# Where the layer norm, turn and router logits of three batches are placed between attention A and the first expert stage

## What is computed

```
x = x + attention_a(layernorm(x))      # linear attention with rotary positions, elu + 1 features
x = x + experts(layernorm(x))          # shared expert + top 2 of 8 routed experts
x = x + attention_b(layernorm(x))      # causal attention with logarithms and softplus
x = x + experts(layernorm(x))          # the same weights again

def experts(xt):                       # xt: 4096 tokens x 128
    shared = (silu(xt @ sg_w.T) * (xt @ su_w.T)) @ sd_w.T
    probs = sigmoid(xt @ router_w.T + routing_bias)
    topk_p, topk_idx = top_k(probs, 2)
    topk_p = topk_p / sum(topk_p)
    # the two chosen experts, each silu(g) * u @ wd, weighted by topk_p
    return shared + routed
```

## Time and profile before

| | |
|---|---|
| median of 3 runs | 1026.67 us (1026.3 to 1032.23) |
| profiled execution | 1028.98 us, its span 1027.1 us |
| mean granted TensorE clock | 0.908 |
| busy: TensorE / its weight load | 80% / 53% |
| busy: VectorE, ScalarE, GpSimd | 72%, 55%, 57% |
| attention A and the shared phase | 0 to about 200 us |
| pairs of the first expert stage | about 200 to 320 us |

### The profile page before, as it was taken

The page is one execution under the profiler, slowest core; times in us unless marked ns, Lnnn a source line. Parts: engine busy times, 40 slices in busy tenths (PEclk is TensorE's granted clock), DMA queues, the critical chain, the costliest instruction groups (busy, mean ns, idle before and its releaser), DMA issues. The chain is left out here.

```text
span 1027.1 us, 19542 instructions
## 1 busy us (share of the span) xinstructions
PE 819.4 (80%) x6459; PEld 545.3 (53%) x6459; DVE 735.8 (72%) x1506; ACT 568.5 (55%) x805; POOL 586.9 (57%) x815
## 2 busy tenths in 40 slices
PE   3887577899986787888888888979796588899890
PEld 2666566799984333333333333333342256799890
DVE  3888745455563658899999998989789646555574
ACT  1454152133334667989898989998763242233230
POOL 2343486881383666666644444455326877788884
PEclk9999588999997878999999999999877688999996
DMA  9990012123338477584737474732210021132444
GB/s 273 300 131 1 16 39 70 54 81 114 101 84 242 124 197 220 150 227 118 234 108 215 116 208 121 224 106 55 70 42 24 32 75 39 40 102 84 132 135 122
DMA packets 114401, 124.00 MB, mean 121 GB/s; under 512 B 13328, under 2 KB 76560, under 8 KB 114176
## 3 DMA queue, kind: packets, MB, share of 16 engines
q1 hardware_dynamic: 96512, 100.80, 36.2%
q0 software_dynamic: 8416, 17.29, 5.4%
q10 hardware_dynamic: 9376, 4.65, 1.6%
HBM read 59.97 MB, written 62.72 MB: 119 GB/s over the span
## 5 line engine op out<-in xcount | busy, mean ns | idle before, releaser
L2070 DVE TENSOR_SCALAR ring_b<-psum 128x1024 int32<-128x1024 int32 x160 | 194.2, 1216 | 24.0 <-PE psum L1765 20.8
L1930 ACT ACTIVATE ring_a<-psum 128x1024 f32<-128x1024 f32 x160 | 162.4, 1021 | 51.0 <-PE psum L1765 45.7
L1936 ACT ACTIVATE ring_b<-ring_b 128x1024 f32<-128x1024 f32 x160 | 168.7, 1055 | 36.5 <-DVE ring_b L2070 36.1
L2198 POOL TENSOR_SCALAR_AFFINE_SELECT ring_b<-ring_b 128x512 f32<-128x512 f32 (+1 forms) x112 | 80.1, 728 | 171.6 <-ACT ring_b L1936 170.9
L1765 PE MATMUL psum<-stacks 32*128 32x128 f32 (+3 forms) x1024 | 98.9, 385 | 66.2 <-DVE ring_b L2070 36.8
L1765 PEld LDWEIGHTS psum<-stacks 32*128 32x128 f32 x1024 | 56.9, 193 | 173.5 <-ACT ring_a L1930 76.6
L2062 DVE TENSOR_SCALAR ring_a<-ring_a 128x1024 f32<-128x1024 f32 x160 | 119.4, 751 | 16.8 <-ACT ring_a L1930 15.0
L949 ACT ACTIVATE ring_b<-psum 128x512 f32<-128x512 f32 x72 | 42.6, 591 | 114.0 <-PE psum L834 88.0
L1818 PE MATMUL psum<-ring_b,values 128*32 128x256 f32 (+3 forms) x1024 | 94.2, 478 | 8.6 <-POOL ring_b L2198 8.6
L1797 PE MATMUL psum<-ring_a,ones_s 128*32 128x256 f32 (+3 forms) x1024 | 92.3, 469 | 9.8 <-POOL ring_a L2198 9.8
L1092 POOL DMA_INDIRECT r_rows<-y_sorted,rows_of x64 | 67.1, 1048 | 51.3 <-DMA y_sorted<-y_out 39.2
(11 more groups left out here) (220 smaller groups left out, 1484.1 us busy)
## 6 DMA issues: line engine op xcount, KB each, us to landing
stack_q<-parts SPq DMA_DIRECT2D x32, 256.0 KB
stack_ky<-parts SPq DMA_DIRECT2D x32, 256.0 KB
stacks<-stack_q SPq DMA_DIRECT2D x64, 128.0 KB
stacks<-stack_ky SPq DMA_DIRECT2D x64, 128.0 KB
stack_k<-parts SPq DMA_DIRECT2D x32, 256.0 KB
stacks<-stack_k SPq DMA_DIRECT2D x64, 128.0 KB
stack_qr<-parts SPq DMA_DIRECT2D x32, 256.0 KB
stacks<-stack_qr SPq DMA_DIRECT2D x64, 128.0 KB
```

Source lines behind the costliest of these rows:

```text
L1930: nc.scalar.activation(exps[:, n % RING, 2 * u:2 * u + 2, :], psum[:, first:first + 2, :], ACT.Exp, scale=SCALE).then_inc(self.exp, 1)
L1936: nc.scalar.activation(part, part, ACT.Ln, bias=1.0).then_inc(self.ln, 1)
L2070: nc.vector.tensor_scalar(ring[:, m % RING, HEADS_B[u][0]:HEADS_B[u][1] + 1, :].bitcast(I32), psum[:, first:first + 2, :].bitcast(I32), 0x ...
L2198: ins = nc.gpsimd.affine_select(out=part, in_=part, pattern=[[0, part.ap[1][1]], [1, 128]], compare_op=ALU.is_ge, fill=0.0, base=0, channe ...
```

## The change

Batches 5, 6 and 7 are handled like batches 1 to 4, in steps 6 to 9 of attention A; only batch 8 stays in the shared phase. `early` becomes 7 for `ffn_1` and with it `first_late` 8 and `scored` 3, so the choice of chunk 1 moves to item 3, ranks, gates, pages and rows to item 4, its page table to item 5. The logits of batch 7 are taken in the shared phase (TensorE at item 1, VectorE at item 2, before `add_shared`). In steps 8 and 9 turn, parts and low part stand behind the attention output. The page table of chunk 0 moves from step 8 to the end of step 9. The powers of batches 5 and 6 are in GpSimd's steps; that of batch 7 comes after 2 sends, that of batch 8 after 12. Batch 8 is normalised on ScalarE behind silu 0, once its bias is there and the logits of batch 7 are taken (the two share a room); its bias is on VectorE behind hidden 0. New waits of TensorE: the turn of batch 6 for the reading of chunk 0's ranks (bank 4), the first down for the logits sum of batch 7, ranks 0 for the logits sum of batch 5. The second expert stage (`led=True`) is unchanged.

```diff
@@ -291,7 +291,7 @@
                 a_project_tokens(pe, 3, w["w_a"][:, 4 * D:5 * D]).then_inc(a_kv, 1)
-            if 1 <= b - AHEAD - 1 <= ffn_1.early:
+            if b <= B and 1 <= b - AHEAD - 1:
                 ffn_1.tensor_logits(pe, b - AHEAD - 1)
@@ -301,14 +301,18 @@
                 a_numerators(pe, b)
-            if b == 8:
+            if b == B:
                 ffn_1.tensor_ranks(pe, 0)
+            if b == B + 1:
+                ffn_1.tensor_logits(pe, b - AHEAD - 1)
             if b < B:
                 a_project_q(pe, b + 1)
-            if 1 <= b - AHEAD <= ffn_1.early:
-                ffn_1.turn(pe, b - AHEAD)
+                if 1 <= b - AHEAD:
+                    ffn_1.turn(pe, b - AHEAD)
             if b > 1:
                 a_output(pe, b)
+            if b >= B:
+                ffn_1.turn(pe, b - AHEAD)
 
@@ -366,7 +370,7 @@
         def a_vector_step(v, b):
-            if 1 <= b - AHEAD <= ffn_1.early:
+            if 1 <= b - AHEAD and b <= B:
                 ffn_1.vector_bias(v, b - AHEAD)
@@ -375,15 +379,17 @@
                 a_rotate(v, b, 1, k_prod, 2, rope_k)
-            if 1 <= b - AHEAD - 1 <= ffn_1.early:
-                ffn_1.vector_logits_of(v, b - AHEAD - 1)
+                if 1 <= b - AHEAD - 1:
+                    ffn_1.vector_logits_of(v, b - AHEAD - 1)
+            else:
+                ffn_1.vector_bias(v, b - AHEAD)
             if b > 1:
...
                 ffn_1.vector_first(v, 0)
-            if b == 8:
+            if b == B:
                 ffn_1.vector_gates(v, 0)
@@ -391,21 +397,22 @@
                 a_feature(v, b, 1, k_prod, k_exp, k_feat)
-            if 1 <= b - AHEAD <= ffn_1.early:
-                ffn_1.vector_low(v, b - AHEAD)
             if b < B:
+                if 1 <= b - AHEAD:
+                    ffn_1.vector_low(v, b - AHEAD)
                 a_rotate_q(v, b + 1)
-            if b == B + 1:
-                ffn_1.vector_bias(v, ffn_1.first_late)
-                ffn_1.vector_stats(v, ffn_1.first_late + 1)
+            else:
+                if b > B:
+                    ffn_1.vector_logits_of(v, b - AHEAD - 1)
             if b > 1:
                 a_add(v, b)
-            if 1 <= b - AHEAD + 1 <= ffn_1.early:
+            if 1 <= b - AHEAD + 1:
                 ffn_1.vector_stats(v, b - AHEAD + 1)
+            if b >= B:
+                ffn_1.vector_low(v, b - AHEAD)
             if b == 7:
                 ffn_1.vector_second(v, 0)
-            if b == 8:
-                ffn_1.vector_stats(v, ffn_1.first_late)
+            if b == B + 1:
                 ffn_1.vector_experts(v, 0)
@@ -442,10 +449,12 @@
                 ffn_1.scalar_exp(a, 0)
-            if 1 <= b - AHEAD <= ffn_1.early:
+            if b < B and 1 <= b - AHEAD:
                 ffn_1.scalar_parts(a, b - AHEAD)
...
                 a_copy_output(a, b)
+            if b >= B:
+                ffn_1.scalar_parts(a, b - AHEAD)
             if b < B:
@@ -467,7 +476,7 @@
                     a_add_turned(p, b + 1, 0)
-                if 1 <= b - AHEAD + 1 <= ffn_1.early:
+                if 1 <= b - AHEAD + 1 and b < B:
                     ffn_1.pool_rstd(p, b - AHEAD + 1)
@@ -478,11 +487,11 @@
                     nc.gpsimd.tensor_tensor(low, whole, high.bitcast(F32), ALU.subtract).then_inc(split_low, 1)
-            sends = (0, 4, 8, 12, 14, 2 * ffn_1.tiles(0))
-            for k in range(len(sends) - 1):
-                ffn_1.send(p, 0, sends[k], sends[k + 1])
-                if ffn_1.first_late + k <= B:
-                    ffn_1.pool_rstd(p, ffn_1.first_late + k)
+            ffn_1.send(p, 0, 0, 2)
+            ffn_1.pool_rstd(p, B - 1)
+            ffn_1.send(p, 0, 2, 12)
+            ffn_1.pool_rstd(p, B)
+            ffn_1.send(p, 0, 12)
 
@@ -579,8 +588,9 @@
                 self.all_pairs, self.all_quads = (PAGES + 1) // 2, (PAGES + 3) // 4
-                self.early = B - chunks[-1]
+                self.early = B - chunks[-1] if led else B - 1
                 self.first_late = self.early + 1
+                self.first_scored = self.first_late if led else self.early
                 self.quads_soon = (2 * chunks[0] * TT - ROUTED + 1) // 4
@@ -711,6 +721,7 @@
                     pe.wait_ge(self.x_low, self.early)
+                    pe.wait_ge(self.logit_ready, self.early)
                     pe.wait_ge(self.chain, self.chain_at(c, RANKS_READ[self.kind(c)]))
@@ -738,6 +749,8 @@
                         pe.wait_ge(self.logit_ready, b - 1)
+                        if not self.led and b == B - AHEAD:
+                            pe.wait_ge(self.chain, self.chain_at(0, RANKS_READ["first"]))
                     elif self.led:
@@ -763,8 +776,8 @@
                 pe.wait_ge(self.chain, self.chain_at(c, CHOSEN))
-                if self.led and c < len(self.chunks) - 1:
-                    pe.wait_ge(self.logit_ready, self.early)
+                if c < len(self.chunks) - 1:
+                    pe.wait_ge(self.logit_ready, self.early if self.led else B - AHEAD - 1)
                 pe.wait_ge(split_low, 1)
@@ -869,7 +882,7 @@
 
-                if self.first_late <= n + self.first_late - 2 <= B:
+                if self.first_scored <= n + self.first_late - 2 <= B:
                     self.tensor_logits(pe, n + self.first_late - 2)
@@ -914,6 +927,8 @@
                 a.wait_ge(self.bias_ready, b)
+                if not self.led and not self.is_early(b):
+                    a.wait_ge(self.logits, self.early)
                 for t in range(TT):
@@ -989,15 +1004,13 @@
                     self.scalar_exp(a, len(self.chunks) - 1)
-                if self.led and self.first_late + n <= B:
+                if self.first_late + n <= B:
                     self.scalar_hat(a, self.first_late + n)
...
                 for n in range(self.offset):
-                    if not self.led and self.first_late + n <= B:
-                        self.scalar_hat(a, self.first_late + n)
                     self.shared_silu(a, self.shared_first[n // IC], n % IC)
@@ -1541,15 +1554,13 @@
                 b = n + self.first_late - 3
-                if self.first_late <= b <= B:
+                if self.first_scored <= b <= B:
                     self.vector_logits_of(v, b)
...
                 last = len(self.chunks) - 1
-                ahead = self.first_late + n + (1 if self.led else 2)
-                if not self.led and ahead - 1 <= B:
-                    self.vector_bias(v, ahead - 1)
+                ahead = self.first_late + n + 1
                 if ahead <= B:
@@ -1571,11 +1582,16 @@
                     self.shared_hidden(v, b, c)
+                    if not self.led and late + n <= B:
+                        self.vector_bias(v, late + n)
                     if self.led and n == 0:
                         self.previous.finish_vector(v)
+                    if not self.led:
+                        self.late_logits(v, n)
                     if n > 0 and c == 0:
                         self.add_shared(v, b - 1)
-                    self.late_logits(v, n)
+                    if self.led:
+                        self.late_logits(v, n)
                     self.late_vector(v, n)
```

## The result

The changed kernel takes 1034.73 us (median of 20 runs, 1030.56 to 1041.31), the kernel before 1028.99 us (20 runs beside it, 1026.11 to 1038.52). The medians differ by 5.7 us; the estimated ratio is 1.0043, 95% interval 1.0022 to 1.0064, that is 4.4 us slower (2.3 to 6.6). The changed kernel is slower, and clear of the scatter, but by less than the 1% that the prediction took as the bound. The profiled execution took 1040.34 us, its span 1038.5 us, one of the slowest of the 20; so its stages are read one by one and not its length.

The account below looks back on a forecast made before the run. VectorE bounds attention, then TensorE's waits and lower clock set when pairs begin; 8 us gained at the choice is given back, +1.5 us on 1026.67 us gives 1028 us, range 1017.5 to 1035.5 us.

Parts of the forecast that it names:

- Steps 6 to 8: Attention, VectorE: step 6 +1.4 us, step 7 +2.4 us, −4.7 us page table and +0.9 us before ninth head mask.
- First gate-up: Start of the shared phase on TensorE, after logits 6 and batch 7's turn: 131.6 against 130.45 us, so +1.2 us.
- GpSimd: Batch 8's power after twelve sends done at 140.9 us; second half's sends resume at 174.5 us, 3.9 us sooner than before.
- New wait at the turn of batch 8: Shared phase, TensorE: waits 7 us, until 142.9 us, for batch 8's normalisation, held by its bias behind GpSimd's power.
- Ranks: Choice of experts ends and ranks are released at 161.6 us, 8 us sooner than before.
- Row numbers behind down 2: Item 4, VectorE: row numbers late by down 2 (3.5 us) and its sum, done at 174.3 us.
- down 3 to 176.9 us: Shared phase, TensorE: down 3, after item 5's hidden product at 174.9 us, ends at 176.9 us.
- Gate-ups 0 and 1: TensorE has done them and logits 7 by 135.9 us; twelve gate-up matmuls take 3.51 us at the full clock.
- A: Clock stays up in steps 8 and 9 as idle pieces shrink: some 6 us less, 1022 us; chance 0.20.
- B: Clock stays down in the shared phase between its waits until 180 us: 8.9 us more, 1037 us; chance 0.11.
- C: Shared-phase chain is shorter than reckoned, batch 8's power or row numbers sooner: gain some 10 us, 1017 us; chance 0.12.
- Behind it: After the first quad: GpSimd's 3.9 us hidden by pairs' slack of some 3.7 us; clearing of value room taken as nothing.

Follow-up runs that it names:

- all four edits: Changed kernel with batch 8's power after 8 sends, page table in item 2, rows before batch 2's sum, batch 7's logit sum in item 1: ratio 0.9949.
- two other kernels: Changed kernel with power after 8 sends, page table in item 2, rows before batch 2's sum, without and with logit sum in item 1: ratios 0.9945, 0.9949.

## Why the prediction was right, and where not

*Overall.* The prediction was 1028 us, +1.5 us over the kernel before; measured were 1034.73 us and +4.4 us by the ratio, in the range and within 1%. Of the 6.7 us between 1028 and 1034.73, 2.3 us are the base (1026.67 us, the median of three runs, where twenty gave 1028.99). The reason was right: what the chain gains, it gives back at the wait for batch 8 and at the row numbers. At the first quad, where the sum ends, the two pairs of profiles show +4.3 and +0.1 us, 2.2 on the mean, against +1.5. The rest of the slowdown lies where the prediction had nothing, or in the scatter; its cause is open.

*Steps 6 to 8.* Right. Step 6 +1.4 us: 12.79 against 11.39 where the clock was up in both profiles. Step 7 +2.4: measured 1.8. Step 8 −3.8: measured −3.77 in the first pair of profiles, −2.7 in the second (13.92 against 16.61 us), where the clock stayed up longer in the kernel before. Head mask of step 8 at 109.2 (108.0), of step 9 at 123.8 (122.6). VectorE sets these steps, and its instructions could be summed.

*First gate-up* +1.2 us: it came at 132.61 and 131.96 against 130.45 and 132.22 us, less than the scatter.

*GpSimd.* Power of batch 8 done at 142.03 us (140.9), the first hidden product just ahead of it at 140.04. Right, and shown by moving it. The second half's sends start at 176.41 us, 1.9 us sooner than before and not 3.9, behind 2.91 us of idle time where almost none was expected: 1.4 us is the late row numbers, and the sum left 0.2 us between row numbers and the first send where both kernels have 0.76.

*New wait at the turn of batch 8.* 6.14 us (7). *Ranks* at 162.72 (161.6). *Row numbers behind down 2.* Done at 175.65 us (174.3), the price 5.1 us when removed: 3.5 us of wait, which was in the sum, and 1.5 us of clock, which was not.

*The step that was mis-sized* is "down 3 to 176.9 us". The sum had the wait in front of it (hidden product at 174.9 us) but priced the down at the full clock, 2.0 us; behind the wait of 3.52 us it took 3.53 us, and 3.68 us in the second profile. The first quad came 2.9 us later than the sum has it (204.07 against 201.2): 1.5 us are this down, and 1.4 us were there when it started (176.30 against 174.9). Those came down the chain from the head mask of step 8, 1.2 us late (109.20 against 108.0), over the first send (120.71 against 119.5) and the power. Gate-ups 0 and 1 were mis-sized too, 4.42 instead of 3.51 us, but cost nothing: TensorE waits for batch 8 behind them until 143.96 us anyway. Nor was the 3.51 us before the change "at the full clock", as the prediction has it: twelve gate-ups take 2.99 to 3.04 us there once nothing disturbs them.

*Rivals.* A, the clock staying up in steps 8 and 9: no, numerators took 2.29 us and the clock is 0.59 at 120 to 140 us. Its mechanism exists, though: the kernel before had the clock up in most of step 8 in its second profile, and the step was 1.75 us shorter. B, the clock down all through: no; it fell at each wait and came back between (gate-ups 3 and 4 took 2.99 us for twelve, at the full clock), so not 8.9 us on top of the sum but the 1.5 us of down 3. The trace shows three waits of over 3 us with the lower clock behind each. The Trainium skill, TensorE: Matmul & The Clock Gate (HAM oscillation), has the loss paid anew at every recurring stall; this trace agrees with it. C, a shorter chain: no for the change as made. With the power sooner, the page table moved and the row numbers first, the stretch is 61.5 us, 8 to 9 us less than before, and the kernel is 0.55% faster; the waits for the choice (6.21 us) and for the turn (1.80 us) are still there.

*Behind it.* GpSimd's gain was hidden, as said; in the kernel with all four edits TensorE has caught up with the sends, and the seventh quad waits 2.37 us.

## What to carry to other kernels

When work is taken off a phase, look which link of the one remaining chain sits behind something foreign in its engine's order: here a power behind twelve sends, row numbers behind an addition that waits for a down. Arriving sooner at a wait that another engine ends gains nothing, and here it cost: with 6.14 us of wait the matmuls behind ran at the lower clock, with 2.13 us they did not. The length alone is no safe guide, since behind waits of 1.80 us in two other kernels they were slow as well. A natural order would be to move the last batch's links first and the batches after that; whether those edits would already help the kernel before, with no batch moved, was not tried. And read a difference of 2 us from more than one profile of each kernel.

## What was not expected

Putting 4.65 us of VectorE work back in front of the first gate-up made the first quad turn 3.3 us sooner: TensorE's wait before the turn fell from 6.14 to 2.13 us, and the clock stayed at 2.4 GHz behind it (gate-up 2 in 1.63 instead of 2.91 us, granted clock 0.90 instead of 0.67 at 140 to 160 us).
